# Moving two ScalarE steps, a GpSimd step and one VectorE step in the attention loop of a decoder layer

## The chip, the cores and the metric

The kernel runs on one core of a Trainium2 chip. A core has five engines with queues of their own: TensorE (PE) multiplies matrices and writes PSUM, VectorE (DVE), ScalarE (ACT) and GpSimd (POOL) work elementwise, SyncE (SP) issues transfers. Each engine runs its own instructions in the order of the program and waits for the others on semaphores. The metric is the device time of one execution in microseconds, lower is better.

## The reference

One decoder layer over 64 sequences of 128 tokens with 256 features: causal self-attention with 16 heads and a position bias, cross-attention to a second input, and a feed-forward part with 8 experts of which each token takes two. Each of the three is added to its input and normalised.

```python
x = _layernorm(x + _L0_attn_ref(x, L0_attn_w_in, L0_attn_w_out))
x = _layernorm(x + _L0_xattn_ref(x, ctx_1024, ctx_1024, Wq, bq, Wk, bk, Wv, bv, Wo, bo))
x = _layernorm(x + _L0_ffn_ref(x, Wr, br, W1, b1, W2, b2))

# the self-attention (the cross-attention has the same form, with biases, no mask, keys and values of ctx)
scores = einsum('bhqd,bhkd->bhqk', q, k) * scale + alibi_bias   # -inf for later keys
out = einsum('ble,fe->blf', einsum('bhqk,bhkd->bhqd', softmax(scores), v), w_out)
```

## The kernel before

Only `attention_layers` is touched; the blocks behind it (logits, routing, experts, last normalisation) are the same in both kernels.

**Tiling.** A group g is 4 tiles of 128 tokens (512 tokens). There are 32 groups: 0 to 15 are the self-attention, 16 to 31 the cross-attention of the same tokens. A group's attention is done in 4 sets, k = 4g + s with s = 0 to 3; a set is two of the tiles (`np_`) and one half of the heads (`half`). A unit u (two tiles, 256 tokens) is what is added to the residual, normalised and stored; group g has units 2g and 2g + 1.

**One step k of the loop**, as TensorE runs it: `turn_max(k)` turns the rounded row maxima, `maxima(k + 1)` computes coarse scores of the next set into the PSUM tensor A, `set_back(k - 2)` turns the weighted values back, then comes a piece of other work; `scores(k)` writes A again, `weigh(k - 1)` multiplies by the values, in odd steps `output_back` turns a unit for the output projection, and another piece of other work ends the step. The half of a step from `maxima` to `scores` is the half-step of the maxima, the rest that of the scores. The pieces of other work belong to the next group (`project_q`, `project_k`, `project_v`, and for cross groups `turn_x`, which turns the residual stream x) or to the group before (`output`, two units late). In step s = 3 they are `project_v(g + 1, 0)`, `project_v(g + 1, 1)` and, where g + 2 is a cross group, `turn_x(g + 2, 0)` at the very end.

**Who answers in a step.** `maxima(k + 1)` is read by VectorE's `reduce_max` (three banks of A, L587; then L589 over ScalarE's copy of the fourth bank; then L595 and L597, which split the maxima into two bf16 parts) and by ScalarE's `copy_bank` (L488). `scores(k)` waits for the first reduction and for that copy, since it overwrites A. ScalarE's `exps` (L495) reads the scores, `copy_o` (L502) frees the bank that `turn_max` needs. In self groups GpSimd clears the future keys behind each `exps` (`clear_future`, L716). VectorE's `normalise_set` (L613, L618) divides by the softmax sums; `output_back` (L365) on TensorE waits for it. ScalarE's `copy_out` (L508) and VectorE's `rest_o` (L623) split the result into two fp32r parts.

**The steps that are moved.** `normalise(u)` (L513, two instructions on ScalarE) normalises a unit; its store on SP waits for it. `source_hi(g)` (L451) rounds the transposed source of a group on ScalarE, `source_lo(g)` (L707) takes the rest on GpSimd; the first projection of group g comes four to five steps later. `take_v(g + 1, i)` (L578 on VectorE, in cross groups) adds the bias to a value projection and frees the PSUM bank B[i]; `turn_x(g + 2, 0)` (L210) writes B[0] and waits for `take_v(g + 1, 0)`; behind it come ScalarE's `turned_x_hi` (L457) and VectorE's `turned_x_lo` (L571). `inverse_deviation(u)` (L723 to L728, four small GpSimd instructions) makes scale and shift for `normalise(u)`.

All orders are written out by hand: each engine's loop over k calls the helpers in the order in which the instructions are queued. Nothing reorders them.

Of the kernel before, what the change touches and what calls it, by code (L numbers as in the profile page):

```python
# [37 lines left out]
def attention_layers(nc, layer_groups, x_in, x_turned, ctx_turned, x1, x2_outs, w_self, w_cross, consts):  # L38


    groups = 2 * layer_groups
    sets = 4 * groups
    halves_of = 2 * groups
    XB = 4
    tag = "at_"
    with ExitStack() as c:
# [74 lines left out]
        def cross(g):  # L121
            return g >= layer_groups

        def layer(g):
            return 1 if cross(g) else 0

        def tx(g, half):

            return 2 * (g - layer_groups) + half
# [315 lines left out]
        @block.scalar  # L445
        def _(act):
            def source_hi(g):
                act.wait_ge(t_loaded[g % 2], 16 * (g // 2 + 1))
                if g >= 2:
                    act.wait_ge(v_full, 2 * (g - 2) + 2)  # L450
                nc.scalar.copy(sT[:, g % 2, 0], turned[:, g % 2]).then_inc(s_hi, 1)  # L451

            def turned_x_hi(g, half):
                act.wait_ge(tx_full, tx(g, half) + 1)
                if half == 0:
                    act.wait_ge(q_full, 2 * (g - 1) + 2)
                nc.scalar.copy(xT[:, 0, half, :], B[half][:, :]).then_inc(tx_hi, 1)  # L457

            def take_q(g, half):
                act.wait_ge(q_full, 2 * g + half + 1)  # L460
                if g >= 2:
                    act.wait_ge(score_full, 4 * (g - 2) + 4)
                for a in range(2):
                    ins = nc.scalar.activation(qp[:, g % 2, half, a, :], B[1][:, :], ACT.Identity,  # L464
                                               bias=q_shift[:, half, a:a + 1] if cross(g) else 0.0,
                                               scale=q_scale[layer(g)][:, a:a + 1])
                ins.then_inc(q_done, 1)

            def take_k(g, half):
                act.wait_ge(k_full, 2 * g + half + 1)  # L470
                if cross(g):
                    ins = nc.scalar.activation(kt[:, g % 2, half, :], B[half][:, :], ACT.Identity, bias=bk[:, half:half + 1])
                else:
                    ins = nc.scalar.copy(kt[:, g % 2, half, :], B[half][:, :])
                ins.then_inc(k_done, 1)

            def take_v(g, i):
                act.wait_ge(v_full, 2 * g + i + 1)
                if g >= 2:
                    act.wait_ge(o_full, 4 * (g - 2) + 4)  # L480
                nc.scalar.copy(v[:, g % 2, 2 * i:2 * i + 2, :, 0:DK],
                               B[i][:, :].rearrange("p (n h d) -> p n h d", n=2, h=H)).then_inc(v_done, 1)

            def copy_bank(k):
                act.wait_ge(max_full, k + 1)
                if k >= 2:
                    act.wait_ge(m2_ready, k - 1)
                nc.scalar.copy(fourth[:, k % 2].rearrange("p c k -> p (c k)"),  # L488
                               A[:, 3].rearrange("p n a k -> p (n a k)")).then_inc(bank_copied, 1)

            def exps(k):
                act.wait_ge(score_full, k + 1)
                if k >= 2:
                    act.wait_ge(o_full, k - 1)
                nc.scalar.activation(pr[:, k % 2].rearrange("p i n a q -> p (i n a q)"),  # L495
                                     A[:].rearrange("p i n a q -> p (i n a q)"), ACT.Exp).then_inc(exp_done, 1)

            def copy_o(k):
                act.wait_ge(o_full, k + 1)
                if k >= 2:  # L500
                    act.wait_ge(t_full, k - 1)
                nc.scalar.copy(oq[:, k % 2, :], C[0][:, :]).then_inc(o_copied, 1)  # L502

            def copy_out(u):
                act.wait_ge(ot_full, u + 1)
                if u >= 2:
                    act.wait_ge(out_full, u - 1)
                nc.scalar.copy(oT[:, u % 2, 0].rearrange("p t n -> p (t n)"), C[1][:, :]).then_inc(ot_hi, 1)  # L508

            def normalise(u):  # L510
                act.wait_ge(shift_done, u + 1)
                for n in range(2):
                    ins = nc.scalar.activation(y[:, u % 4, n, :], y[:, u % 4, n, :], ACT.Identity,  # L513
                                               bias=shift[:, u % 2, n:n + 1], scale=rstd[:, u % 2, n:n + 1])
                ins.then_inc(y_ready, 1)

            source_hi(0)
            act.wait_ge(small_in, 16)
            take_q(0, 0)
            take_k(0, 0)  # L520
            take_q(0, 1)
            take_k(0, 1)
            take_v(0, 0)
            take_v(0, 1)
            source_hi(1)
            copy_bank(0)
            for k in range(sets):
                g, s = divmod(k, 4)
                more = g + 1 < groups
                if k + 1 < sets:  # L530
                    copy_bank(k + 1)
                if s == 0 and more and cross(g + 1):
                    if g + 1 == layer_groups:
                        act.wait_ge(made, 1)
                    turned_x_hi(g + 1, 1)
                elif s == 1 and more:
                    take_k(g + 1, 0)
                elif s == 3 and more and not cross(g + 1):
                    take_v(g + 1, 0)
                exps(k)  # L540
                if k >= 1:
                    copy_o(k - 1)
                if k % 2 == 1 and k >= 3:
                    copy_out((k - 3) // 2)
                if s == 0 and more:
                    take_q(g + 1, 0)
                elif s == 1 and more:
                    take_q(g + 1, 1)
                elif s == 2 and more:
                    take_k(g + 1, 1)  # L550
                elif s == 3 and more:
                    if not cross(g + 1):
                        take_v(g + 1, 1)
                    if g + 2 < groups:
                        source_hi(g + 2)
                        if cross(g + 2):
                            turned_x_hi(g + 2, 0)
                if s == 1 and g >= 1:
                    normalise(2 * g - 2)
                elif s == 3 and g >= 1:  # L560
                    normalise(2 * g - 1)
            copy_o(sets - 1)
            copy_out(halves_of - 1)
            normalise(halves_of - 2)
            normalise(halves_of - 1)

        @block.vector
        def _(dve):
# [105 lines left out]
            for k in range(sets):  # L674
                g, s = divmod(k, 4)
                more = g + 1 < groups
                take_max(k)
                if k + 1 < sets:
                    reduce_max(k + 1)
                if k >= 2:  # L680
                    normalise_set(k - 2)
                if s == 0 and more and cross(g + 1):
                    turned_x_lo(g + 1, 1)
                if s == 0 and g >= 1:
                    residual(2 * g - 2)
                if s == 2 and g >= 1:
                    residual(2 * g - 1)
                if k % 2 == 1 and k >= 3:
                    rest_o((k - 3) // 2)
                if s == 3 and more and cross(g + 1):  # L690
                    take_v(g + 1, 0)
                    take_v(g + 1, 1)
                if s == 3 and g + 2 < groups and cross(g + 2):
                    turned_x_lo(g + 2, 0)
# [7 lines left out]
        def _(pool):  # L702
            nc.gpsimd.memset(minus_half[:], -0.5).then_inc(eps_done, 1)

            def source_lo(g):
                pool.wait_ge(s_hi, g + 1)
                nc.gpsimd.tensor_tensor(sT[:, g % 2, 1], turned[:, g % 2], sT[:, g % 2, 0].bitcast(FP32), ALU.subtract).then_inc(s_lo, 1)  # L707
# [37 lines left out]
            for k in range(sets):  # L745
                g, s = divmod(k, 4)
                if not cross(g):
                    clear_future(k)
                if s == 0 and g + 1 < groups and cross(g + 1):
                    add_bias(g + 1)  # L750
                if s == 0 and g >= 1:
                    inverse_deviation(2 * g - 2)
                if s == 2 and g >= 1:
                    inverse_deviation(2 * g - 1)
                if s == 3 and g + 2 < groups:
                    source_lo(g + 2)
                if k == 5:
                    split_cross()
# [923 lines left out]
```

## Time and profile before

| | |
|---|---|
| median of 3 runs | 1737.83 us (1737.78 to 1737.97) |
| profiled execution, device time | 1737.31 us |
| its span, first to last instruction | 1735.6 us |
| TensorE busy | 1463.6 us, 84% |
| VectorE, ScalarE, GpSimd busy | 1054.5, 970.5, 632.2 us |
| attention (the part that is changed) | from the start to about 980 us |

The profile lists instructions by line of the program and engine. A wait is the idle time of an engine in front of an instruction, with the instruction that released it. A timeline row gives the start, the duration, the engine, the line, the operation, what is written and read, how many are merged in the row, and in brackets the idle time before it and its releaser. PEld is TensorE's weight load, which overlaps the multiplication; "issue" means that the profile shows no releaser.

### The profile page before, as it was taken

The numbers are of one execution on the slowest core, as the hardware profiler recorded it, in microseconds if no ns is written. First come the engines' busy times: TensorE is split into PE (matmuls) and PEld (weight loads), VectorE is DVE, ScalarE is ACT, GpSimd is POOL, SyncE is SP. The second block draws the span as 40 slices with busy tenths as digits, with TensorE's granted clock in tenths as the row PEclk, the third lists the DMA queues.
The fourth block names the chain that finished last, engine by engine and source line by source line (L and its number), as shares of the span: only waits on it lengthen the run. The fifth ranks groups of instructions, "written<-read, shape, count | busy, mean of one in ns | idle before, by whom it ended". The sixth has DMA issues, their size and how long they took to land. (4 is left out here: it accounts for less than half of the span.)

```text
span 1735.6 us, 43611 instructions
## 1 busy us (share of the span) xinstructions
PE 1463.6 (84%) x17896; PEld 1214.8 (70%) x17896; DVE 1054.5 (61%) x2277; ACT 970.5 (56%) x1419; POOL 632.2 (36%) x615
## 2 busy tenths in 40 slices
PE   5999999999999999999998591223999999999950
PEld 4777777777777777777776341223999999999950
DVE  3666666666667677767766347794544454455425
ACT  3677767777766666676765220012655555555507
POOL 1544444444432222322230000055254455454326
PEclk9999999999999999999999795555999999999985
DMA  5011112112112222222111341004334433442229
GB/s 178 20 57 57 57 57 63 58 56 68 45 52 67 75 75 75 74 74 75 63 60 38 126 116 12 0 0 134 83 58 96 97 81 61 96 98 45 28 53 357
DMA packets 129795, 129.54 MB, mean 75 GB/s; under 512 B 28288, under 2 KB 116464, under 8 KB 129600
## 3 DMA queue, kind: packets, MB, share of 16 engines
q1 hardware_dynamic: 114496, 106.29, 19.6%
q0 software_dynamic: 15104, 20.48, 7.1%
q8 instruction: 143, 2.34, 0.5%
q14 instruction: 52, 0.43, 0.1%
HBM read 82.54 MB, written 44.20 MB: 73 GB/s over the span
## 5 line engine op out<-in xcount | busy, mean ns | idle before, releaser
L495 ACT ACTIVATE at_pr<-at_A 128x2048 f32<-128x2048 f32 x128 | 240.7, 1880 | 196.4 <-PE at_A L325 196.4
L587 DVE TENSOR_REDUCE at_mx<-at_A 128x12 f32<-128x1536 f32 x128 | 224.6, 1755 | 32.7 <-PE at_A L292 27.1
L34 PE MATMUL ex_D<-ex_w,ex_hT 128*128 128x256 f32 (+1 forms) x1920 | 233.8, 281 | 0.4
L34 PEld LDWEIGHTS ex_D<-ex_w,ex_hT 128*128 128x128 f32 (+1 forms) x1920 | 230.5, 184 | 3.1 <-DVE ex_raw L1426 1.9
L34 PE MATMUL ex_U<-ex_xT,ex_w 128*128 128x384 f32 (+1 forms) x1152 | 222.1, 352 | 0.0
L1482 POOL DMA_INDIRECT total<-ex_o,ex_ids x80 | 131.6, 1645 | 228.0 <-DVE ex_o L1431 196.3
L34 PEld LDWEIGHTS ex_U<-ex_xT,ex_w 128*128 128x128 f32 x1152 | 207.2, 189 | 7.4
L716 POOL TENSOR_SCALAR_AFFINE_SELECT at_pr<-at_pr 128x2048 f32<-128x2048 f32 x64 | 128.5, 2008 | 225.2 <-ACT at_pr L495 225.2
L1416 DVE TENSOR_TENSOR ex_hT<-ex_h,ex_hT 128x384 fp32r<-128x384 f32 (+1 forms) x192 | 112.6, 587 | 97.0 <-ACT ex_hT L1376 97.0
L623 DVE TENSOR_TENSOR at_oT<-at_C,at_oT 128x512 fp32r<-128x512 f32 x64 | 44.3, 692 | 178.0 <-ACT at_oT L508 178.0
L325 PE MATMUL at_A<-at_qp,at_kt 32*128 32x256 f32 x2048 | 142.5, 392 | 0.0
L341 PE MATMUL at_C<-at_pr,at_v 128*32 128x128 f32 x4096 | 139.2, 277 | 1.0 <-ACT at_oq L502 1.0
L341 PEld LDWEIGHTS at_C<-at_pr,at_v 128*32 128x32 f32 x4096 | 104.6, 110 | 43.7 <-issue 42.4
L1375 ACT ACTIVATE ex_h<-ex_U,ex_b 128x384 f32<-128x384 f32 (+1 forms) x192 | 116.7, 608 | 25.5 <-PE ex_U L34 21.4
L707 POOL TENSOR_TENSOR at_sT<-at_turned,at_sT 128x1024 fp32r<-128x1024 f32 x32 | 75.8, 2369 | 126.7 <-ACT at_sT L451 126.7
L1376 ACT ACTIVATE ex_hT<-ex_U,ex_b 128x384 fp32r<-128x384 f32 (+1 forms) x192 | 115.2, 600 | 0.0
L1466 POOL DMA_INDIRECT ex_xg<-rows,ex_ids x80 | 102.1, 1276 | 35.2 <-issue 22.6
L1348 ACT CAST ex_xT<-ex_T 128x384 fp32r<-128x384 f32 (+1 forms) x48 | 21.9, 510 | 165.4 <-PE ex_T L1299 165.4
L723 POOL TENSOR_SCALAR at_shift<-at_mv 128x2 f32<-128x2 f32 x64 | 14.8, 231 | 269.5 <-DVE at_mv L649 266.9
L34 PE MATMUL at_B<-at_wo,at_oT 128*128 128x256 f32 x768 | 108.1, 290 | 1.9 <-DVE at_oT L623 1.4
L34 PE MATMUL at_B<-at_sT,at_wk 128*128 128x512 f32 x384 | 105.8, 411 | 1.4 <-ACT at_qp L464 1.4
L34 PE MATMUL at_B<-at_wv,at_sT 128*128 128x256 f32 x768 | 106.7, 288 | 0.0
(189 smaller groups left out, 2703.3 us busy)
## 6 DMA issues: line engine op xcount, KB each, us to landing
ex_w_in<-in_w SPq DMA_DIRECT2D x16, 1024.0 KB, 6.8
at_turned<-in_x_turned SPq DMA_DIRECT2D x16, 512.0 KB, 4.0
at_x<-in_x SPq DMA_DIRECT2D x16, 512.0 KB, 3.7
x<-at_y SPq DMA_DIRECT2D x32, 256.0 KB, 2.2
at_x<-x SPq DMA_DIRECT2D x16, 512.0 KB, 3.7
at_turned<-in_ctx_turned SPq DMA_DIRECT2D x16, 512.0 KB, 4.1
rows<-at_y SPq DMA_DIRECT2D x32, 256.0 KB, 2.2
total<-at_y SPq DMA_DIRECT2D x32, 256.0 KB, 2.8
```

Source lines behind the costliest of these rows:

```text
L34: last = nc.tensor.matmul(out, pick_l(left, a), pick_r(right, b), start=(start and n == 0), stop=(stop and n == 2))
L325: last = nc.tensor.matmul(A[:, i, n, :, :], kt[rows, g % 2, half, tok], qp[rows, g % 2, half, :, tok], start=False, stop=(n == 1), skip_gr ...
L341: last = nc.tensor.matmul(b[32 * j:32 * j + VW, (2 * n + quad) * P:(2 * n + quad + 1) * P], v[:, g % 2, 2 * np_ + n, half * HEADS_HALF + 4 ...
L495: nc.scalar.activation(pr[:, k % 2].rearrange("p i n a q -> p (i n a q)"), A[:].rearrange("p i n a q -> p (i n a q)"), ACT.Exp).then_inc(e ...
L587: nc.vector.tensor_reduce(mx[:, k % 2, 0:12], A[:, 0:3].rearrange("p i n a k -> p (i n a) k"), AX, ALU.max).then_inc(max_done, 1)
L707: nc.gpsimd.tensor_tensor(sT[:, g % 2, 1], turned[:, g % 2], sT[:, g % 2, 0].bitcast(FP32), ALU.subtract).then_inc(s_lo, 1)
L716: nc.gpsimd.affine_select(out=t, in_=t, compare_op=ALU.is_ge, fill=0.0, base=0, pattern=[[0, 16], [1, P]], channel_multiplier=-1).then_inc ...
L1375: nc.scalar.activation(h[:, m % HR, 0:n], U[m % UP][:, 0:n], ACT.Silu, bias=b1[:, j, m:m + 1])
L1376: nc.scalar.activation(hT[:, par(j, ch), 0, m, 0:n], U[m % UP][:, 0:n], ACT.Silu, bias=b1[:, j, m:m + 1]).then_inc(u_done, 1)
L1416: nc.vector.tensor_tensor(hT[:, par(j, ch), 1, m, 0:n], h[:, m % HR, 0:n], hT[:, par(j, ch), 0, m, 0:n].bitcast(FP32), ALU.subtract).then_ ...
L1466: nc.gpsimd.indirect_dma_start(xg[0:n, xg_of(s), b, :], None, rows_dram, bass.IndirectOffsetOnAxis(ap=ids[0:n, e, at:at + 1], axis=0), bou ...
L1482: nc.gpsimd.indirect_dma_start(sum_dram, bass.IndirectOffsetOnAxis(ap=ids[0:n, e, at:at + 1], axis=0), o[0:n, pr, b, :], None, bounds_chec ...
```

## The change

ScalarE: `normalise(2g - 2)` went behind everything else in step s = 1 and `normalise(2g - 1)` in step s = 3 of group g. Now the first stands in step s = 2, between `copy_bank` and `exps`, and the second between `copy_bank` and `exps` of step s = 0 of the group after. `source_hi(g + 2)` goes from the end of step s = 3 to step s = 2, between `copy_bank` and `normalise`. GpSimd: `source_lo(g + 2)` goes from the end of step s = 3 to the end of step s = 2. VectorE: in step s = 3, `take_v(g + 1, 0)` goes ahead of `rest_o`; `take_v(g + 1, 1)` stays behind it. No instruction is added or removed, and TensorE's and SP's orders stay as they were.

```diff
@@ ScalarE, loop over k
                 elif s == 3 and more and not cross(g + 1):
                     take_v(g + 1, 0)
+                if s == 0 and g >= 2:
+                    normalise(2 * g - 3)
+                elif s == 2:
+                    if g + 2 < groups:
+                        source_hi(g + 2)
+                    if g >= 1:
+                        normalise(2 * g - 2)
                 exps(k)
...
                     if not cross(g + 1):
                         take_v(g + 1, 1)
-                    if g + 2 < groups:
-                        source_hi(g + 2)
-                        if cross(g + 2):
-                            turned_x_hi(g + 2, 0)
-                if s == 1 and g >= 1:
-                    normalise(2 * g - 2)
-                elif s == 3 and g >= 1:
-                    normalise(2 * g - 1)
+                    if g + 2 < groups and cross(g + 2):
+                        turned_x_hi(g + 2, 0)
+            normalise(halves_of - 3)
             copy_o(sets - 1)
@@ VectorE, loop over k
+                if s == 3 and more and cross(g + 1):
+                    take_v(g + 1, 0)
                 if k % 2 == 1 and k >= 3:
                     rest_o((k - 3) // 2)
                 if s == 3 and more and cross(g + 1):
-                    take_v(g + 1, 0)
                     take_v(g + 1, 1)
@@ GpSimd, loop over k
-                if s == 3 and g + 2 < groups:
+                if s == 2 and g + 2 < groups:
                     source_lo(g + 2)
```

What now stands in the rows, in the three places that matter below. First GpSimd in a self group: L723 to L728 are `inverse_deviation`, L716 is `clear_future`, L707 `source_lo`. Before, from the `inverse_deviation` of step s = 2 on:

```order
L723 TENSOR_SCALAR at_shift<-at_mv 128x2
L724 TENSOR_SCALAR at_rstd<-at_mv 128x2
L726 TENSOR_TENSOR at_rstd<-at_rstd,at_minus_half 128x2
L728 TENSOR_TENSOR at_shift<-at_shift,at_rstd 128x2
L716 AFFINE_SELECT at_pr<-at_pr 128x2048
L707 TENSOR_TENSOR at_sT<-at_turned,at_sT 128x1024
L716 AFFINE_SELECT at_pr<-at_pr 128x2048
```

The same stretch of GpSimd in the changed kernel, whose lines stand 3 further down (L726 to L731 `inverse_deviation`, L719 `clear_future`, L710 `source_lo`):

```order
L726 TENSOR_SCALAR at_shift<-at_mv 128x2
L727 TENSOR_SCALAR at_rstd<-at_mv 128x2
L729 TENSOR_TENSOR at_rstd<-at_rstd,at_minus_half 128x2
L731 TENSOR_TENSOR at_shift<-at_shift,at_rstd 128x2
L710 TENSOR_TENSOR at_sT<-at_turned,at_sT 128x1024
L719 AFFINE_SELECT at_pr<-at_pr 128x2048 x2
```

`source_lo` moved ahead of one `clear_future` and now follows `inverse_deviation` directly.

VectorE in step s = 3 of a cross group, before: L589 to L597 end `reduce_max`, L613 and L618 are `normalise_set`, L623 `rest_o`, L578 the two `take_v`, L571 `turned_x_lo`.

```order
L589 TENSOR_REDUCE at_mx<-at_fourth 128x4
L595 CAST at_m2<-at_mx 128x8x2
L597 TENSOR_TENSOR at_m2<-at_mx,at_m2 128x8x2
L613 RECIPROCAL at_rden<-at_C1 128x16
L618 TENSOR_TENSOR at_on<-at_C1,at_rden 128x2x128
L623 TENSOR_TENSOR at_oT<-at_C1,at_oT 128x512
L578 TENSOR_TENSOR at_v<-at_B0,at_bv 128x32x16
L578 TENSOR_TENSOR at_v<-at_B1,at_bv 128x32x16
L571 TENSOR_TENSOR at_xT<-at_B0,at_xT 128x512
```

And VectorE at the same place of the changed kernel, whose lines stand 2 further down:

```order
L591 TENSOR_REDUCE at_mx<-at_fourth 128x4
L597 CAST at_m2<-at_mx 128x8x2
L599 TENSOR_TENSOR at_m2<-at_mx,at_m2 128x8x2
L615 RECIPROCAL at_rden<-at_C1 128x16
L620 TENSOR_TENSOR at_on<-at_C1,at_rden 128x2x128
L580 TENSOR_TENSOR at_v<-at_B0,at_bv 128x32x16
L625 TENSOR_TENSOR at_oT<-at_C1,at_oT 128x512
L580 TENSOR_TENSOR at_v<-at_B1,at_bv 128x32x16
L573 TENSOR_TENSOR at_xT<-at_B0,at_xT 128x512
```

The first `take_v` changed places with `rest_o`.

ScalarE in a self group, from the last `take_v` of step s = 3 (L481) to the `exps` of step s = 0 (L495), before: L451 is `source_hi`, L513 `normalise`, L488 `copy_bank`.

```order
L508 CAST at_oT<-at_C1 128x512
L481 COPY at_v<-at_B1 128x32x16
L451 CAST at_sT<-at_turned 128x1024
L513 ACTIVATE at_y<-at_y,at_shift,at_rstd 128x256 x2
L488 COPY at_fourth<-at_A 128x512
L495 ACTIVATE at_pr<-at_A 128x2048
```

ScalarE at that place of the changed kernel (the lines of these helpers are the same):

```order
L508 CAST at_oT<-at_C1 128x512
L481 COPY at_v<-at_B1 128x32x16
L488 COPY at_fourth<-at_A 128x512
L513 ACTIVATE at_y<-at_y,at_shift,at_rstd 128x256 x2
L495 ACTIVATE at_pr<-at_A 128x2048
```

`copy_bank` went to the front, `normalise` behind it, and `source_hi` left this place for step s = 2.

## Rows read from the trace of the kernel before

**Rows 1.** Stretches: length, busy PE, PEld, DVE, ACT, POOL, TensorE clock, DMA share, GB/s.

```profile
60.00:490.00 430.00, 423.66 (x6838) 325.74 (x6837) 289.37 (x606) 303.73 (x406) 208.70 (x207) 1.00 0.18 55
530.00:950.00 420.00, 387.94 (x6034) 303.94 (x6031) 294.39 (x614) 284.88 (x374) 99.73 (x138) 0.99 0.21 67
...
940.00:955.00 15.00, 11.42 (x191) 8.47 (x186) 9.21 (x21) 7.44 (x9) 1.35 (x4) 0.77 0.11 36
```

**Rows 2.** Waits of PE over the span: total us, times, longest.

```profile
PE at_B L210 <- DVE at_v L578: 20.5, 15, 1.4
...
PE at_A L319 <- ACT at_fourth L488: 7.9, 29, 0.3
```

**Rows 3.** Timeline, self group, join of steps s = 3 and s = 0.

```profile
314.38 1.05 ACT L451 CAST at_sT<-at_turned 128x1024 fp32r<-128x1024 f32 x1
...
314.81 1.76 DVE L587 TENSOR_REDUCE at_mx<-at_A 128x12 f32<-128x1536 f32 x1
...
315.33 1.09 ACT L513 ACTIVATE at_y<-at_y,at_shift,at_rstd 128x256 f32<-128x256 f32 x2
...
316.32 0.57 ACT L488 COPY at_fourth<-at_A 128x512 f32<-128x512 f32 x1
...
317.04 0.41 PE L319 MATMUL at_A<-at_mT,at_sel 32*128 32x128 bf16 x16 [0.27 <-ACT at_fourth L488]
```

**Rows 4.** Timeline, cross group, end of step s = 3 and start of s = 0.

```profile
724.05 1.68 PE L34 MATMUL at_B<-at_wv,at_sT 128*128 128x256 f32 x12
...
725.65 0.69 DVE L623 TENSOR_TENSOR at_oT<-at_C,at_oT 128x512 fp32r<-128x512 f32 x1 [2.77 <-ACT at_oT L508]
726.26 1.28 DVE L578 TENSOR_TENSOR at_v<-at_B,at_bv 128x512 f32<-128x512 f32 x2
...
727.09 0.63 PE L210 MATMUL at_B<-at_ident,at_x 128*128 128x128 f32 x4 [1.35 <-DVE at_v L578]
...
728.37 0.69 DVE L571 TENSOR_TENSOR at_xT<-at_B,at_xT 128x512 fp32r<-128x512 f32 x1 [0.83 <-ACT at_xT L457]
```

**Rows 5.** Timeline, two places where L595 or L597 falls into a GpSimd TENSOR_TENSOR.

```profile
59.35 2.38 POOL L707 TENSOR_TENSOR at_sT<-at_turned,at_sT 128x1024 fp32r<-128x1024 f32 x1 [0.65 <-ACT at_sT L451]
...
61.04 0.72 DVE L595 CAST at_m<-at_mx 128x16 bf16<-128x16 f32 x1
...
76.30 1.28 POOL L737 TENSOR_TENSOR at_wk<-at_w_cross_in,at_wk 128x512 fp32r<-128x512 f32 x1
76.40 1.21 DVE L597 TENSOR_TENSOR at_m<-at_mx,at_m 128x16 bf16<-128x16 f32 x1
```

**Rows 6.** Timeline, self group, step s = 3: GpSimd, VectorE and the output's turning.

```profile
309.46 0.20 POOL L728 TENSOR_TENSOR at_shift<-at_shift,at_rstd 128x2 f32<-128x2 f32 x1
...
310.00 0.17 DVE L595 CAST at_m<-at_mx 128x16 bf16<-128x16 f32 x1
...
310.59 0.42 DVE L618 TENSOR_TENSOR at_on<-at_C,at_rden 128x256 f32<-128x256 f32 x1
...
311.77 0.66 PE L365 MATMUL at_C<-at_ident,at_on 128*128 128x128 f32 x4
```

**Rows 7.** Timeline, step s = 3: L728 of group 15, then a cross group.

```profile
482.10 0.20 POOL L728 TENSOR_TENSOR at_shift<-at_shift,at_rstd 128x2 f32<-128x2 f32 x1
...
719.70 0.20 POOL L728 TENSOR_TENSOR at_shift<-at_shift,at_rstd 128x2 f32<-128x2 f32 x1
...
721.87 0.17 DVE L595 CAST at_m<-at_mx 128x16 bf16<-128x16 f32 x1
...
723.64 0.66 PE L365 MATMUL at_C<-at_ident,at_on 128*128 128x128 f32 x4
```

**Rows 8.** Timeline, cross group, ScalarE from step s = 1 to the `exps` of s = 2.

```profile
713.23 1.08 ACT L513 ACTIVATE at_y<-at_y,at_shift,at_rstd 128x256 f32<-128x256 f32 x2
714.22 0.58 ACT L488 COPY at_fourth<-at_A 128x512 f32<-128x512 f32 x1
...
716.32 1.88 ACT L495 ACTIVATE at_pr<-at_A 128x2048 f32<-128x2048 f32 x1 [1.53 <-PE at_A L325]
```

## The prediction

> **What bounds the kernel now.** I read the table of stretches first. Over the self-attention TensorE is busy 423.66 of 430 us, over the cross-attention 387.94 of 420, both at a granted clock of 0.99 to 1.00 (2.4 GHz); VectorE and ScalarE stand near 70% in both [rows 1]. So TensorE sets the pace, and a change elsewhere is worth what it takes from, or adds to, TensorE's waits. The list of TensorE's waits has two that this change can reach. In the cross groups `turn_x` (L210) waits for `take_v` on VectorE: 20.5 us in 15 waits. `scores` (L319) waits for ScalarE's copy of the fourth bank: 7.9 us in 29 waits [rows 2]. The rest of the reading is in the timeline at those two places and at one where no wait stands today.
>
> **Part 1, ScalarE.** At the join of steps s = 3 and s = 0 ScalarE does `source_hi` (1.05 us) and the two instructions of `normalise` (1.09 us) before the copy, which so starts at 316.32, 1.5 us after VectorE's reduction of the same maxima began at 314.81. `scores` starts at 317.04 with 0.27 us of idle time put down to the copy [rows 3]. With the copy first, the reduction ends last, at 314.81 + 1.76 = 316.57; TensorE's piece of output projection ends at 317.04 - 0.27 = 316.77. So the whole 0.27 us goes, and what is late next is VectorE, 0.2 us earlier and hidden. The same holds where `normalise` stood at the end of s = 1: in the cross groups that pushed the copy to 714.22 [rows 8]. In all, the change takes the 7.9 us of the 29 waits [rows 2]: **-7.9 us**.
>
> What was moved must fit elsewhere. The tightest place is s = 2 of a cross group. ScalarE gets to the copy at 713.23 instead of 714.22; then come the copy (0.58), `source_hi` (1.05) and `normalise` (1.08): 715.94, or some 0.3 us less, since ScalarE's starts lie closer than its durations (713.23 to 714.22 is 0.99 for 1.08). `exps` starts at 716.32 today, having waited 1.53 us for TensorE [rows 8], and at 716.05 with `scores` 0.27 us earlier. It fits, with 0.1 to 0.4 us to spare. Cover gone, each 0.1 us would cost 0.1 us, because `copy_o` behind `exps` opens the next step. In step s = 0 only `normalise` is added, half as much. On SP the store of the odd unit and the load of the next source, queued behind it, come out at the same place of step s = 0 as before (there too `normalise` had just ended), and the load has more than a step until the new `source_hi` wants it. These moves I cost at nothing.
>
> **Part 2, VectorE.** In a cross group TensorE ends its last value projection at 724.05 + 1.68 = 725.73 and starts `turn_x` only at 727.09, when the first of the two L578 (1.28 us for both, from 726.26) is done. VectorE had been idle for 2.77 us before `rest_o` at 725.65, waiting for ScalarE [rows 4]. The moved `take_v` needs only the projection before, so it falls into this idle time, and `turn_x` follows the projection directly: 1.35 us less idle, and up to 1.5 with weights loaded ahead. What is late next is VectorE's own chain: `rest_o`, the other `take_v`, then `turned_x_lo` (L571). It starts at 728.37 after 0.83 us of idle time. In the new order it can start at 726.26 + 0.64 = 726.90, when the second `take_v` is done, and ScalarE's half of that step, 0.64 us from the end of `turn_x`, is ready by then: 1.47 us earlier. The row after it, the next reduction, follows at once. Both chains move by about the same, so I take 1.45 us for each of 15 waits: **-21.8 us** (bounds 1.35 and 1.53, or -20.3 to -23.0).
>
> **Part 3, GpSimd, the part that costs.** `source_lo` (L707, 2.38 us) now follows `inverse_deviation` in the queue. In the trace VectorE's L595 normally takes 0.17 us [rows 6]. Where it falls into L707 (59.35 to 61.73) it takes 0.72 us and ends at 61.76; where L597 falls into GpSimd's L737 (76.30 to 77.58) it takes 1.21 us and ends at 77.61 [rows 5]. Both end 0.03 us behind GpSimd's instruction: they do not run slower, they wait it out. VectorE's other work beside GpSimd shows no such stretch: the reduction L587 takes 1.76 us with L707 beside it [rows 3], the usual time.
>
> The Trainium skill has a rule for this: in SBUF — State Buffer, section "SBUF: two separate sides", VectorE and GpSimd share one pair of SBUF ports as an exclusive lock, whoever starts first keeps it for the whole instruction, and it is wanted by VectorE's two-port modes and by its operations with two SBUF inputs. L595 is a copy within SBUF, L597 has two SBUF inputs, so the trace agrees; by the rule alone the wait would also be the rest of GpSimd's instruction.
>
> Before, `source_lo` ran across the join to s = 0. Now, in a self group, L728 ends at 309.66, L707 runs to 309.66 + 2.38 = 312.04, and L595 arrives at 310.00: it ends at 312.07 instead of 310.17, 1.90 us late. L618 ends at 311.01 today, so at 312.91, and TensorE's `output_back` (L365), which needs it, starts at about 312.95 instead of 311.77 [rows 6]. That is close to 1.2 us of a wait that does not exist today, with `project_v`, queued behind L365 and all of the next step behind that. I take 1.17. The groups where the rows stand like this are 2 to 14, 13 of them: groups 0 and 1 differ (no unit to turn yet, and GpSimd late by the splitting of the cross weights). In group 15 L728 ends at 482.30 [rows 7], a little later against VectorE; L595 or L597 then waits to the end of L707 at 484.68, 1.4 us for TensorE by the same sum. Together 13 x 1.17 + 1.4 = **+16.6 us**.
>
> In cross groups there is no `clear_future`, so GpSimd is free earlier: L707 runs from 719.90 to 722.28, L595 at 721.87 waits 0.4 us, L618 ends 0.84 us behind it as in the self group (310.17 to 311.01 [rows 6]), at 723.15, and L365 is due at 723.64 [rows 7]. Hidden, by 0.5 us; nothing.
>
> **The sum.** -7.9 - 21.8 + 16.6 = -13.1 us on the profiled execution's 1737.31 us: 1724.2. The median, 1737.83, lies 0.5 us above that execution: 1724.7, rounded 1724.5. So the self-attention gets slower by some 13 us and the cross-attention faster by some 26.
>
> Its own range. The terms' bounds: part 2 from -20.3 to -23.0; part 3 from 14 x 1.0 = 14 (GpSimd starting at once, a little overlap) to 14 x 1.4 = 19.6. The end of the attention has stretches at half clock (1.2 GHz): from 940 to 955 us the granted clock was 0.77 on average, 0.23 x 15 = 3.5 us lost [rows 1]. A shift of 13 us can move such a stretch onto busy or idle work, there or at the start of the experts, so I allow 3.5 us either way. That gives 1715 to 1731.
>
> **The rivals.** (a) The wait in part 3 does not reach TensorE: GpSimd starts its instruction only after L595 and L597, or lets them through. For it: GpSimd's L707 starts only 0.34 us ahead of L595, and spans on GpSimd are rough. Against it: L597 follows L595 directly and would be caught in its place, and all stretched rows end with GpSimd's. Then -29.7 us: 1708.1.
> (b) Slower than before: the cross groups' gain fails to come through, since VectorE's order, and not `turn_x`, sets the start of `scores` in s = 0. The place is `turned_x_lo`, which must follow `rest_o` and the second `take_v`. If that keeps its time, part 2 is worth 0 and the rest is 16.6 - 7.9 = +8.7: 1746.5. It decides from the point where `turned_x_lo` gains less than 8.7 / 15 = 0.58 us. Against it: the row shows 0.83 us of idle time before it and its releaser is the chain behind `turn_x` [rows 4].
> (c) Within 0.2%: ScalarE's queue in s = 2 overruns its 0.1 to 0.4 us of slack by 0.4 us in each of 29 groups, +11.6 us: 1736.3. For it: the slack is thin. Against it: 2.13 us are put in where 0.99 us of `normalise` ahead of the copy fall away and `exps` has waited 1.53 us [rows 8].
>
> **How the numbers follow.** The forecast with its range has 0.80, (a) 0.08, (b) 0.05, (c) 0.04, and 0.03 is left for a clock that is granted otherwise on a self-attention that now waits, split over the sides (the cross-attention waits as long today, at 0.99 [rows 1]). Differences under 0.2%, 3.5 us, I count as no change, about what a measurement of this kernel can tell. Faster: 0.80 + 0.08 + 0.01 = 0.89; same 0.05; slower 0.06. The range 1715 to 1731 is the forecast's own and holds 0.8.
>
> **What would show it.** In the changed trace, `turn_x` has no wait on `take_v`; the 29 waits for the fourth bank are gone; a new wait of TensorE's L365 on VectorE's L618 stands there 14 times with about 1.2 us (PE and weight loads), 16 to 17 us in all, none of it in cross groups. L595 shows 2.07 us in self steps s = 3, ending with `source_lo`. A self group takes 1.17 - 0.27 = 0.9 us longer, a cross group 1.45 + 0.27 = 1.7 us less. The prediction is wrong if L365 starts on time in the self groups (a), or if VectorE's reduction in s = 0 of the cross groups moves less than `turn_x` (b), or if ScalarE's `exps` of s = 2 follows `normalise` without idle time (c).

## The result

| | before | after |
|---|---|---|
| median | 1737.8 us | 1716.34 us |
| range of the runs | 1733.5 to 1738.0 | 1715.9 to 1718.9 |
| profiled execution: time, span | 1737.31, 1735.6 us | 1715.96, 1714.2 us |

The ratio is 0.9884, with a 95% interval from 0.9869 to 0.9900: 21.5 us faster, where 13.3 were forecast. The range, 1715 to 1731, holds it near its lower end.

**The two stages.** The stretches of the changed kernel, for [rows 1] (length, busy PE, PEld, DVE, ACT, POOL, TensorE clock, DMA share, GB/s):

```profile
60.00:490.00 430.00, 416.08 (x6747) 318.39 (x6750) 304.65 (x597) 301.99 (x399) 201.71 (x204) 1.00 0.19 55
530.00:950.00 420.00, 402.32 (x6359) 316.25 (x6358) 307.14 (x651) 301.43 (x394) 103.46 (x150) 1.00 0.23 70
918.00:933.00 15.00, 10.19 (x217) 7.88 (x220) 10.90 (x23) 7.36 (x9) 1.35 (x4) 1.00 0.14 49
```

TensorE gets through fewer instructions in the 430 us of the self-attention (6747 for 6838) and more in the 420 us of the cross-attention (6359 for 6034). The two stages moved in opposite directions, as forecast.

**TensorE's waits**, first in the self-attention (60 to 500 us), then one of the list over the whole span, for [rows 2]:

```profile
PE at_C L365 <- DVE at_on L620: 14.9, 14, 1.3
```

```profile
PE at_C L365 <- DVE at_on L620: 16.9, 15, 2.0
```

The waits of L210 for `take_v` and of L319 for the fourth bank are on neither list any more. `output_back` (L365) has 14 new ones; the 15th, of 2.0 us, stands in both kernels at the very end of the attention.

**The new wait**, in the timeline of a self group, for [rows 6] (the changed kernel's lines: L731 ends `inverse_deviation`, L710 is `source_lo`, L597 and L599 the two that split the maxima, L620 ends `normalise_set`):

```profile
313.28 0.20 POOL L731 TENSOR_TENSOR at_shift<-at_shift,at_rstd 128x2 f32<-128x2 f32 x1
...
313.43 2.37 POOL L710 TENSOR_TENSOR at_sT<-at_turned,at_sT 128x1024 fp32r<-128x1024 f32 x1
...
313.83 2.00 DVE L597 CAST at_m<-at_mx 128x16 bf16<-128x16 f32 x1
...
315.86 0.17 DVE L599 TENSOR_TENSOR at_m<-at_mx,at_m 128x16 bf16<-128x16 f32 x1
...
316.24 0.42 DVE L620 TENSOR_TENSOR at_on<-at_C,at_rden 128x256 f32<-128x256 f32 x1
...
316.72 0.66 PE L365 MATMUL at_C<-at_ident,at_on 128*128 128x128 f32 x4 [1.05 <-DVE at_on L620]
```

A cast of 16 columns takes 2.00 us. It ends at 315.83, 0.03 us behind `source_lo` (313.43 + 2.37 = 315.80), and L365 waits for 1.05 us. In groups 2 to 14 it is this cast that is held up; in group 15 it is the subtraction behind it, L599, which takes 2.22 us.

**The join of s = 3 and s = 0** in a self group, for [rows 3]:

```profile
319.76 0.59 ACT L488 COPY at_fourth<-at_A 128x512 f32<-128x512 f32 x1 [0.33 <-PE at_A L292]
319.76 1.76 DVE L589 TENSOR_REDUCE at_mx<-at_A 128x12 f32<-128x1536 f32 x1 [0.49 <-PE at_A L292]
...
320.24 1.09 ACT L513 ACTIVATE at_y<-at_y,at_shift,at_rstd 128x256 f32<-128x256 f32 x2
...
321.65 0.40 PE L319 MATMUL at_A<-at_mT,at_sel 32*128 32x128 bf16 x16
```

The copy starts with the reduction instead of 1.5 us behind it, and L319 starts 1.89 us after the reduction's start instead of 2.23.

**The end of step s = 3 in a cross group**, for [rows 4] (L580 is `take_v`, L625 `rest_o`, L573 `turned_x_lo`):

```profile
716.45 0.68 DVE L580 TENSOR_TENSOR at_v<-at_B,at_bv 128x512 f32<-128x512 f32 x1
...
717.71 1.68 PE L34 MATMUL at_B<-at_wv,at_sT 128*128 128x256 f32 x12
...
719.22 0.60 PE L210 MATMUL at_B<-at_ident,at_x 128*128 128x128 f32 x4
719.31 0.69 DVE L625 TENSOR_TENSOR at_oT<-at_C,at_oT 128x512 fp32r<-128x512 f32 x1 [2.18 <-ACT at_oT L508]
...
720.51 0.68 DVE L573 TENSOR_TENSOR at_xT<-at_B,at_xT 128x512 fp32r<-128x512 f32 x1
```

`turn_x` now starts 1.51 us after the last value projection's start (before: 727.09 - 724.05 = 3.04), `turned_x_lo` 2.80 instead of 4.32.

**Step s = 2 of a cross group**, for [rows 8]:

```profile
707.20 0.58 ACT L488 COPY at_fourth<-at_A 128x512 f32<-128x512 f32 x1
707.67 1.06 ACT L451 CAST at_sT<-at_turned 128x1024 fp32r<-128x1024 f32 x1
...
708.61 1.10 ACT L513 ACTIVATE at_y<-at_y,at_shift,at_rstd 128x256 f32<-128x256 f32 x2
...
709.96 1.88 ACT L495 ACTIVATE at_pr<-at_A 128x2048 f32<-128x2048 f32 x1 [0.25 <-PE at_A L325]
```

`exps` still waits 0.25 us for TensorE: the two moved steps fit.

**Where the 21.9 us up to the last `exps` come from**, by the starts of `exps` in the profiled executions, against the forecast's terms:

| stretch | before | after | difference | forecast |
|---|---|---|---|---|
| start to group 2 | 90.8 | 89.4 | -1.3 | -0.3 |
| groups 2 to 13 | 341.5 | 350.4 | +8.9 | 12 x 0.90 = +10.8 |
| groups 14, 15 | 60.5 | 60.2 | -0.3 | about +0.9 |
| groups 16 to 29 | 419.3 | 392.8 | -26.5 | 14 x -1.72 = -24.1 |
| group 30 to the last `exps` | 48.3 | 45.5 | -2.7 | -0.3 |

The forecast's terms are put where their waits stand in the trace before; they add up to its -13. From the last `exps` to the end the changed kernel takes 0.6 us more.

### The profile page after: what moved, and what is told of

Its sections match the earlier page's. It is cut to its first block and busy times, and to the rows that moved or that the text cites. A ratio compares the mean times of both kernels' runs of the same rounds, so it can differ in the third digit from the quotient of the medians.

```text
span 1714.2 us, 43611 instructions
## 1 busy us (share of the span) xinstructions
PE 1455.4 (85%) x17896; PEld 1208.5 (71%) x17896; DVE 1073.8 (63%) x2277; ACT 975.7 (57%) x1419; POOL 630.5 (37%) x615
## 5 line engine op out<-in xcount | busy, mean ns | idle before, releaser
L495 ACT ACTIVATE at_pr<-at_A 128x2048 f32<-128x2048 f32 x128 | 240.7, 1881 | 152.6 <-PE at_A L325 152.6
L589 DVE TENSOR_REDUCE at_mx<-at_A 128x12 f32<-128x1536 f32 x128 | 224.6, 1755 | 37.7 <-PE at_A L292 33.7
L34 PE MATMUL ex_D<-ex_w,ex_hT 128*128 128x256 f32 (+1 forms) x1920 | 233.8, 282 | 0.4
L34 PEld LDWEIGHTS ex_D<-ex_w,ex_hT 128*128 128x128 f32 (+1 forms) x1920 | 230.4, 184 | 3.1 <-DVE ex_raw L1429 1.9
L34 PE MATMUL ex_U<-ex_xT,ex_w 128*128 128x384 f32 (+1 forms) x1152 | 221.7, 351 | 0.0
L719 POOL TENSOR_SCALAR_AFFINE_SELECT at_pr<-at_pr 128x2048 f32<-128x2048 f32 x64 | 128.5, 2007 | 241.2 <-ACT at_pr L495 241.2
L34 PEld LDWEIGHTS ex_U<-ex_xT,ex_w 128*128 128x128 f32 x1152 | 206.9, 189 | 7.3
L625 DVE TENSOR_TENSOR at_oT<-at_C,at_oT 128x512 fp32r<-128x512 f32 x64 | 44.3, 692 | 146.2 <-ACT at_oT L508 146.2
L1351 ACT CAST ex_xT<-ex_T 128x384 fp32r<-128x384 f32 (+1 forms) x48 | 21.9, 510 | 165.3 <-PE ex_T L1302 165.3
L726 POOL TENSOR_SCALAR at_shift<-at_mv 128x2 f32<-128x2 f32 x64 | 14.8, 231 | 258.7 <-DVE at_mv L651 256.1
L34 PE MATMUL at_B<-at_wo,at_oT 128*128 128x256 f32 x768 | 108.0, 290 | 1.4 <-DVE at_oT L625 1.4
L1429 DVE TENSOR_TENSOR ex_raw<-ex_D,ex_b 128x256 f32<-128x256 f32 x80 | 33.8, 423 | 118.3 <-PE ex_D L34 118.0
L34 PE MATMUL at_B<-at_wv,at_sT 128*128 128x256 f32 x768 | 106.8, 289 | 0.0
L34 PE MATMUL at_B<-at_sT,at_wk 128*128 128x512 f32 x384 | 105.6, 410 | 1.4 <-ACT at_qp L464 1.4
```

The lines of the kernel that those rows point to most:

```text
L34: last = nc.tensor.matmul(out, pick_l(left, a), pick_r(right, b), start=(start and n == 0), stop=(stop and n == 2))
L589: nc.vector.tensor_reduce(mx[:, k % 2, 0:12], A[:, 0:3].rearrange("p i n a k -> p (i n a) k"), AX, ALU.max).then_inc(max_done, 1)
L625: nc.vector.tensor_tensor(oT[:, u % 2, 1].rearrange("p t n -> p (t n)"), C[1][:, :], oT[:, u % 2, 0].rearrange("p t n -> p (t n)").bitcast ...
L719: nc.gpsimd.affine_select(out=t, in_=t, compare_op=ALU.is_ge, fill=0.0, base=0, pattern=[[0, 16], [1, P]], channel_multiplier=-1).then_inc ...
```

## The experiments

Two theories had to be told apart for the loss: GpSimd's long instruction holds up VectorE's small ones and through them TensorE, or ScalarE's and VectorE's new order does. For the gain it was open whether VectorE's move alone brings it. A group's length, from the starts of `exps`, is the finest measure, so here it is for all profiled executions (mean us per group). E7 to E9 ran on another chip, where the kernel before took 1735.4 us and not 1737.4 to 1737.8, so their medians are to be compared through the ratio:

| kernel | median us | ratio to before, 95% | groups 2 to 13 | groups 16 to 29 |
|---|---|---|---|---|
| before | 1737.8 | | 28.46 | 29.95 |
| changed | 1716.3 | 0.9884 (0.9869 to 0.9900) | 29.20 | 28.06 |
| E1 `source_lo` back in s = 3 | 1702.0 | 0.9793 (0.9774 to 0.9813) | 28.08 | 28.14 |
| E2 VectorE's move alone | 1728.5 | 0.9952 (0.9935 to 0.9968) | 28.46 | 29.48 |
| E3 without VectorE's move | 1740.1 | 1.0018 (1.0007 to 1.0029) | 29.21 | 29.59 |
| E4 `source_lo` in quarters | 1701.5 | 0.9794 (0.9778 to 0.9811) | 28.09 | 28.07 |
| E5 `source_lo` in halves | 1715.4 | 0.9872 (0.9855 to 0.9888) | 29.13 | 28.06 |
| E6 two more copies in s = 2 | 1732.9 | 0.9977 (0.9964 to 0.9990) | 29.60 | 28.74 |
| E7 as E2, `add_bias` in quarters | 1722.2 | 0.9920 (0.9899 to 0.9940) | 28.47 | 29.01 |
| E8 `normalise` as before | 1722.4 | 0.9917 (0.9898 to 0.9935) | 29.24 | 28.40 |
| E9 E4 and `add_bias` in quarters | 1704.7 | 0.9818 (0.9800 to 0.9835) | 28.08 | 28.30 |

### E1: `source_lo` back to step s = 3

Edit, against the changed kernel:

```diff
-                if s == 2 and g + 2 < groups:
+                if s == 3 and g + 2 < groups:
                     source_lo(g + 2)
```

> The changed kernel with GpSimd's `source_lo` back in step s = 3, behind that step's `clear_future`; all else of the change stays. Theory (GpSimd's instruction holds up the cast of the maxima in s = 3 of the self groups): the cast is back at 0.17 us, TensorE's L365 has none of its 14 waits (14.9 us, and 1.13 us a group with the late start), and the time is 1716.3 - 15.8 = 1700.5 us, between 1699 and 1703. Rival (the wait of L365 comes from ScalarE's or VectorE's new order, GpSimd only stands beside it): no change, 1715 to 1718.

Measured: 1702.0 us, self groups 28.08 instead of 29.20. TensorE's waits from 60 to 500 us:

```profile
PE at_B L34 <- DVE at_xT L573: 1.2, 1, 1.2
PE at_C L355 <- issue: 0.3, 1, 0.3
```

None of the 14 waits of L365 is left. One line of GpSimd's order cost 1.12 us in each self group. By their lengths the 14 groups take 15.8 us less; group 16, to which the one wait of 1.2 us belongs, takes 1.1 more; by the medians it is 14.3 in all.

The cross groups keep their gain: 28.14 us, of which 0.08 is group 16's. The timeline of one shows why (L731 ends `inverse_deviation`, L710 is `source_lo`, L714 `add_bias`, which adds the output bias to x):

```profile
700.31 0.19 POOL L731 TENSOR_TENSOR at_shift<-at_shift,at_rstd 128x2 f32<-128x2 f32 x1
700.46 2.38 POOL L710 TENSOR_TENSOR at_sT<-at_turned,at_sT 128x1024 fp32r<-128x1024 f32 x1
708.60 2.39 POOL L714 TENSOR_TENSOR at_x<-at_x,at_bo 128x1024 f32<-128x1024 f32 x1 [5.76 <-PE at_B L210]
```

There `source_lo` follows `inverse_deviation` directly in either order, since no `clear_future` lies between them, and it can start at once because ScalarE's `source_hi` is done. So in the cross groups GpSimd's moved line did nothing; it was a cost alone, in the self groups.

### E4 and E5: `source_lo` in four pieces, and in two

E4 writes the same subtraction as four instructions of 256 columns at its place in s = 2, E5 as two of 512:

```diff
-                nc.gpsimd.tensor_tensor(sT[:, g % 2, 1], turned[:, g % 2], ...).then_inc(s_lo, 1)
+                for q in range(4):
+                    t, c = q // 2, slice(q % 2 * 256, q % 2 * 256 + 256)
+                    ins = nc.gpsimd.tensor_tensor(sT[:, g % 2, 1, t, c], turned[:, g % 2, t, c], ...)
+                ins.then_inc(s_lo, 1)
```

> The changed kernel with `source_lo` written as four GpSimd instructions of 256 columns each at the same place, same work. Theory (a VectorE instruction waits for the end of the one GpSimd instruction that runs, then goes): the cast and the subtraction behind it wait for at most a quarter each, 0.6 us, so the set is normalised at most 1.2 us late and 0.7 in the mean, TensorE's L365 waits 0 to 0.2 us: 1701 to 1704 us. Rival (both engines slow each other down over the 2.4 us, or VectorE waits until GpSimd has no work queued): as before, 1715 to 1718.

> The changed kernel with `source_lo` as two GpSimd instructions of 512 columns each at the same place. Theory (each VectorE instruction of the two waits for the end of the one GpSimd instruction then running): the cast ends with the first half, the subtraction is caught by the second and ends with it, so TensorE's L365 keeps its wait of about 1.1 us in the self groups: 1715 to 1718 us. Rival (only the cast is held up, the subtraction is not): the wait ends 1.2 us earlier and L365 is on time: 1701 to 1703.

Measured: 1701.5 us with quarters, 1715.4 with halves. First the timeline with halves, then with quarters (in a timeline row x2 or x4 merges the pieces):

```profile
314.78 2.51 POOL L711 TENSOR_TENSOR at_sT<-at_turned,at_sT 128x512 fp32r<-128x512 f32 x2
315.18 0.90 DVE L597 CAST at_m<-at_mx 128x16 bf16<-128x16 f32 x1
316.12 1.21 DVE L599 TENSOR_TENSOR at_m<-at_mx,at_m 128x16 bf16<-128x16 f32 x1
...
318.00 0.66 PE L365 MATMUL at_C<-at_ident,at_on 128*128 128x128 f32 x4 [0.99 <-DVE at_on L620]
```

```profile
308.33 2.80 POOL L712 TENSOR_TENSOR at_sT<-at_turned,at_sT 128x256 fp32r<-128x256 f32 x4
308.73 0.36 DVE L597 CAST at_m<-at_mx 128x16 bf16<-128x16 f32 x1
309.12 0.65 DVE L599 TENSOR_TENSOR at_m<-at_mx,at_m 128x16 bf16<-128x16 f32 x1
...
310.51 0.66 PE L365 MATMUL at_C<-at_ident,at_on 128*128 128x128 f32 x4
```

With halves the cast is let go at 316.08, in the middle of GpSimd's 2.51 us, and the subtraction behind it is caught by the second half: it ends at 317.33, 0.04 behind GpSimd. With quarters each waits out one quarter and L365 is on time, although GpSimd is busy for 0.4 us longer. So it is neither a slowing of both engines nor a wait for an empty queue: a VectorE instruction of these two kinds waits for the end of the one GpSimd instruction that is running. Both expectations held, but for group 15 of E5: there L365 waits only 0.18 us.

### E2 and E3: VectorE's move alone, and the rest alone

E2 is the kernel before with `take_v(g + 1, 0)` ahead of `rest_o`, the second hunk of the change. E3 is the changed kernel with that hunk undone.

> The kernel before with VectorE's move alone: `take_v(g + 1, 0)` ahead of `rest_o` in the cross groups. Theory (the whole of TensorE's late start of `turn_x` comes back, weights' loading and VectorE's chain behind it included, 1.51 us in each of 15 groups and 0.6 in group 30): 1737.8 - 23.3 = 1714.5 us. Rival as in the prediction's lower bound (1.35 us of idle time each, nothing in group 30): 1717.5. Rival (b) of the prediction (VectorE's chain keeps its time): 1737.

> The changed kernel without VectorE's move: ScalarE's and GpSimd's moves alone. If the parts add: 1716.3 + 23.3 = 1739.6, so 1738 to 1742, slightly slower than the kernel before or the same: self groups 0.75 us longer each, cross groups 0.35 shorter each. If the cross groups' gain beyond VectorE's move (0.38 a group where 0.27 was forecast) needs both moves together, the cross groups gain 0.27 here.

E3 came as expected, 1740.1 us: the rest alone costs a little. In its list (60 to 950 us) L210 and L365 both wait:

```profile
PE at_B L210 <- DVE at_v L580: 19.8, 15, 1.4
PE at_C L365 <- DVE at_on L620: 14.9, 14, 1.3
```

E2 missed: 1728.5 us, where 1714.5 was expected. The cross groups get shorter by 0.47 us each instead of 1.5. `turn_x` no longer waits, but from 530 to 950 us TensorE has two waits of L34 that neither kernel has there, the first of `project_q` for `turned_x_lo`, the second of the output projection in step s = 3:

```profile
PE at_B L34 <- DVE at_xT L571: 11.5, 13, 0.9
...
PE at_B L34 <- issue: 2.9, 13, 0.2
```

The timeline of E2 at one of the first kind (L708 is `source_lo`, L712 `add_bias`, L595 the cast, L571 `turned_x_lo`):

```profile
724.45 2.39 POOL L708 TENSOR_TENSOR at_sT<-at_turned,at_sT 128x1024 fp32r<-128x1024 f32 x1 [6.76 <-ACT at_sT L451]
...
726.79 2.36 POOL L712 TENSOR_TENSOR at_x<-at_x,at_bo 128x1024 f32<-128x1024 f32 x1
...
728.07 1.11 DVE L595 CAST at_m<-at_mx 128x16 bf16<-128x16 f32 x1
...
729.94 0.68 DVE L571 TENSOR_TENSOR at_xT<-at_B,at_xT 128x512 fp32r<-128x512 f32 x1
...
730.76 1.61 PE L34 MATMUL at_B<-at_xT,at_wq 128*128 128x512 f32 x6 [0.89 <-DVE at_xT L571]
```

It is the same kind of wait in another place. `source_lo` has waited 6.76 us for ScalarE's `source_hi`, which is still at the join; so, with TensorE and VectorE 1.5 us ahead, `add_bias` starts only behind `source_lo` and runs until 729.15; the cast falls into it and ends at 729.18. In the kernel before, VectorE's cast came just as `add_bias` ended. By the steps, 0.81 us of the 1.51 are lost again here, from s = 0 to s = 1 (7.24 us instead of 6.43), and 0.23 in step s = 3 (8.35 instead of 8.12), where `source_hi` stands ahead of `turned_x_hi` on ScalarE. So the parts don't add: taken singly they are worth 0.47 (E2) and 0.36 us (E3) of a cross group, together 1.89.

### E7 and E8: what stands in VectorE's way

E7 is E2 with `add_bias` in four instructions of 256 columns each. E8 is the changed kernel with `normalise` back at the ends of steps s = 1 and s = 3, so that VectorE's, `source_hi`'s and `source_lo`'s moves are left:

```diff
-                if s == 0 and g >= 2:
-                    normalise(2 * g - 3)
-                elif s == 2:
-                    if g + 2 < groups:
-                        source_hi(g + 2)
-                    if g >= 1:
-                        normalise(2 * g - 2)
+                if s == 2 and g + 2 < groups:
+                    source_hi(g + 2)
                 exps(k)
...
+                if s == 1 and g >= 1:
+                    normalise(2 * g - 2)
+                elif s == 3 and g >= 1:
+                    normalise(2 * g - 1)
```

> VectorE's move alone, as before, and GpSimd's `add_bias` (x + bo, one instruction of 128x1024 in step s = 0 of the cross groups) written as four of 128x256. Theory (in the kernel with VectorE's move alone, `source_lo` pushes `add_bias` back until it catches VectorE's cast of the maxima, which takes 1.11 us there, and through `turned_x_lo` `project_q` waits 0.89 us in 15 groups): the cast waits for a quarter at most, the step from s = 0 to s = 1 goes from 7.26 back to 6.43 us, 14 x 0.83 = 11.6 us: 1728.5 - 11.6 = 1716.9, between 1715 and 1719. Rival (what holds VectorE's move down is ScalarE, whose `source_hi` and `normalise` stand between `turned_x_hi` and the rest): no change, 1727 to 1730.

> The changed kernel with `normalise` where it was before (ends of steps s = 1 and s = 3): VectorE's move and the moves of `source_hi` and `source_lo` to s = 2. Theory (`source_lo` out of the way of `add_bias` is what lets the cross groups have VectorE's whole 1.5 us; `normalise` is worth only the 0.34 us of s = 2): cross groups 28.06 + 0.34 = 28.4 us each, self groups within 0.1 of 29.2, 1716.3 + 14 x 0.34 = 1721 us, between 1720 and 1723. Rival (`normalise` had to leave the join as well): cross groups near 29.4, 1733 to 1736.

E8 came out as expected: 1722.4 us, cross groups at 28.40 us. With `source_hi` and `source_lo` away from the join the cross groups have VectorE's whole gain, and `normalise` is worth 0.34 us of s = 2. Together with E1, where GpSimd's line alone is undone and the gain stays, this puts it down to `source_hi`, for which `source_lo` waits by the program: it is the one move besides VectorE's that both runs have. No run has these two moves alone.

E7 went the way of the theory but half as far: 1722.2 us instead of 1716.9, and 29.01 us a cross group. Its timeline says why:

```profile
721.60 2.80 POOL L713 TENSOR_TENSOR at_x<-at_x,at_bo 128x256 f32<-128x256 f32 x4
...
722.88 0.17 DVE L595 CAST at_m<-at_mx 128x16 bf16<-128x16 f32 x1
723.09 0.65 DVE L597 TENSOR_TENSOR at_m<-at_mx,at_m 128x16 bf16<-128x16 f32 x1
...
725.11 1.63 PE L34 MATMUL at_B<-at_xT,at_wq 128*128 128x512 f32 x6 [0.41 <-DVE at_xT L571]
```

The cast gets through, the subtraction is caught by a quarter (0.65 instead of 0.18 us), and TensorE has no slack here: its wait falls from 0.89 to 0.41 us. The expectation had left out that a quarter catches the second one. ScalarE's `source_hi` and `normalise` at the join, the rival, are unchanged in E7 and can't be what fell. What they hold down is the 0.23 us of step s = 3, which E7 has lost as E2 has (8.35 us) and E8, with `normalise` at the join but not `source_hi`, has back (8.11).

### E6: two more copies in step s = 2

```diff
                     if g >= 1:
                         normalise(2 * g - 2)
+                    act.wait_ge(bank_copied, k + 2)
+                    for i in range(2):
+                        nc.scalar.copy(extra[:, i], fourth[:, (k + 1) % 2].rearrange("p c k -> p (c k)"))
                 exps(k)
```

> The changed kernel with two more ScalarE copies of 128x512 (0.47 us each from start to start, their output unused) in every step s = 2 between `normalise` and `exps`, to find what the cover there is worth. `exps` of s = 2 now waits 0.53 us for TensorE in self groups and 0.25 in cross groups. Theory (behind `exps` comes `copy_o`, and `turn_max` of the next step waits for it, so what goes beyond the cover costs its full size): 0.94 - 0.53 = 0.41 in 16 groups and 0.94 - 0.25 = 0.69 in 16: 6.6 + 11 = 17.6 us, 1732 to 1736. Rival (TensorE has other work queued that takes it up): under 3 us, 1716 to 1720.

Measured: 1732.9 us, self groups longer by 0.40 and cross groups by 0.68 us (expected 0.41 and 0.69). From 60 to 950 us TensorE's longest total wait is now that of `turn_max` for `copy_o`:

```profile
PE at_C L304 <- ACT at_oq L503: 17.0, 31, 1.6
```

So the cover in s = 2 (the time for which ScalarE would wait for TensorE anyway) was real and thin, and beyond it ScalarE's time there counts in full.

### E9: both GpSimd steps in quarters

E4 with `add_bias` in four instructions too.

> A candidate for the best version: the changed kernel with both `source_lo` and `add_bias` in four GpSimd instructions each. Theory: as with `source_lo` alone in quarters (1701.5), and group 16, where `add_bias` catches a cast, falls from 28.2 towards 28.05: 1701 to 1702 us, which can't be told from it. Rival (more GpSimd instructions cost on the path): 1703 to 1706.

1704.7 us, cross groups 28.30 us for 28.07 in E4: worse, as the rival had it, and not the 1701 to 1702 of the theory. The four pieces take 2.80 us instead of 2.38, so `add_bias` now reaches the cast that it had just missed, and `project_q` waits again (530 to 950 us):

```profile
PE at_B L34 <- DVE at_xT L573: 4.1, 13, 0.3
```

The best versions are E1 and E4, 1702.0 and 1701.5 us, which can't be told apart; both beat the kernel before by 2.1% and the change by 0.8 to 0.9%. E1 costs one line.

## Why the prediction was right, and where it was off

**Right, step by step.** The wait that the trace before didn't have came in the 14 groups named, 14 times and none in a cross group, by the mechanism named: GpSimd's `source_lo` catches VectorE's cast (in group 15 the subtraction), which ends 0.03 us behind it. L597 takes 2.00 us where 2.07 was written down. E1 shows by removal that it costs 1.12 us a group (forecast 1.17), E4 and E5 that its unit is one GpSimd instruction. VectorE's move and ScalarE's copy gave what their waits said and more; `exps` in s = 2 kept 0.25 us of slack (forecast 0.1 to 0.4), and E6 shows the price beyond it. Rival (a), GpSimd without effect, 1708, and rival (b), no gain in the cross groups, are out; rival (c) too.

**Partly by luck inside the range.** The range was to be the sum of its terms' bounds: part 2 from -20.3 to -23.0, part 3 from 14 to 19.6, 3.5 us of clock either way. With part 1 and the median of before these give 1717.4 to 1732.7, and not the 1715 to 1731 that stand there. The measured 1716.3 lies in the stated range and 1 us below the one that the terms give. The mechanisms were right, and the sizes were off by more than was allowed for.

**What the sum had too small or left out** makes up the 8 us between 13.3 and 21.5 (the differences by step are from the profiled executions):

- ScalarE's part. It was sized at TensorE's idle time, 0.27 us at each of 29 places. The step from s = 3 to s = 0 shrank by 0.33 us in the self groups (7.51 to 7.18 in E1) and the step into s = 2 by 0.34 in the cross groups; and 0.05 us came in the self groups' s = 2, where no L488 wait was listed, and 0.35 in step s = 2 of group 1. Together some 2.7 us.
- VectorE's part, 1.45 us taken, 1.51 measured (9.64 to 8.12 from s = 3 to s = 0): 0.9 us. Step s = 3 of group 30, which has no wait of L210 and so was not in the sum, gained 0.6 us as well (8.12 to 7.52); E2 has this gain and E3 has not.
- GpSimd's part, 1.17 taken, 1.12 measured: 0.8 us.
- A step not in the sum: in group 14 `source_hi` also stood in front of `turned_x_hi`, and the output projection waited 0.54 us. The step shrank from 9.08 to 8.13 us in E1: 0.9 us, for which the sum had nothing.
- The clock, some 2.4 us. Over 15 us at the start of the last group it was granted at 0.77 before [rows 1], and at 1.00 over the stretch 22 us earlier in the changed kernel. E1, whose orders in the last group are the changed kernel's, was granted 0.77 from 907 to 922 us and takes 19.8 us for the last three steps, where the changed kernel takes 18.0: so 1.75 of the 1.8 us that these steps gained are the clock. At the start 0.6 us of the 1.3 were gained between the first two `exps`, beside a stretch at half clock that both kernels have (0.83 on average from 20 to 40 us) and that came 1.3 us earlier in the changed one. The range allowed for the clock with 3.5 us either way, the sum had nothing. Like the kernel before, all nine experiments have a half-clock stretch that starts 9 to 16 us ahead of the last `exps`; only the profiled execution of the changed kernel has none. I take that for an accident of this execution and not for a gain of the change; where these stretches lay in its other three runs is not on record.

These come to some 8.3 us, of which 0.6 are lost again behind the last `exps`.

**Right with a gap in the argument.** The prediction added its parts, and for this change the sum held because all of them were made. E2 shows that VectorE's term was not a property of VectorE's move: with `source_hi` left at the join, and `source_lo` behind it, it would have been a third. The step that failed to see this is "the row after it, the next reduction, follows at once": it followed the path to the reduction and stopped before the cast behind it, though `add_bias` on GpSimd was on the very next rows. The wait that the prediction found in the self groups was also waiting in the cross groups, and the change happened to clear it, which is luck too. The prediction had costed the move of `source_hi` at nothing and looked for no gain in it; by E1 and E8 it is what lets the cross groups have VectorE's gain, while GpSimd's moved line only costs.

## What to carry to other kernels

When a long GpSimd instruction is moved, look not at its consumers, which here had a step to spare, but at which small VectorE copies and two-operand instructions it will run beside: a cast of 0.17 us can take 2 us, and what waits behind it pays. Cutting the GpSimd instruction helps where the victims have slack for a piece each, and hurts where the longer total reaches a victim it had missed. Gains from moves on several engines are to be worked out together: making two engines earlier can put a third one's instruction in their way.

## What the runs showed of the hardware

- Not all of VectorE's work is held up. Beside `source_lo` the reductions keep their time, also L591, which reads SBUF (0.67 to 0.68 us with and without), and the statistics L643, 0.75 us beside the splitting of the weights at 78.87 us. Held up were the cast within SBUF and the subtraction with two SBUF inputs, whichever came while GpSimd's instruction ran.
- Cutting a GpSimd instruction of 2.38 us costs little: 2.51 us in two pieces and 2.80 in four, about 0.14 us for each more.
- A wait on TensorE costs more than its idle time in the list: 0.33 to 0.34 us where 0.27 was listed, 1.51 where 1.35 was, and 1.12 where 1.05 is. The rows of the weight loads of `turn_x` show a part of the reason, in the kernel before and in the changed one. With the wait the loading starts 0.04 us ahead of the multiplication (727.09), when the wait is over; without it 0.27 us ahead of the end of the projection (719.39), and the multiplication starts 0.17 us ahead of that end:

```profile
727.05 0.42 PEld L210 LDWEIGHTS at_B<-at_ident,at_x 128*128 128x128 f32 x4 [1.53 <-issue]
```

```profile
719.12 0.46 PEld L210 LDWEIGHTS at_B<-at_ident,at_x 128*128 128x128 f32 x4
```
